# Order of centring, turning and draining in the two channel layer norms of a spectral-convolution and expert block

## The reference, cut to what matters

```python
def _ln_c(v, eps=1e-06):                # over the 32 channels of a pixel
    m = jnp.mean(v, axis=1, keepdims=True)
    s = jnp.var(v, axis=1, keepdims=True)
    return (v - m) / jnp.sqrt(s + eps)

x = x + spectral_conv(_ln_c(x))         # 2D FFT, weights per mode, inverse FFT
t = tokens(x); t = t + experts(_ln_t(t))    # 16 experts, 8 tokens each
x = x + sweeps(_ln_c(x))                # 4 recurrent 1D convolutions over rows and columns
t = tokens(x); t = t + experts(_ln_t(t))
```

## Time and profile before

| | us |
|---|---|
| median of three runs | 591.21 |
| lowest and highest run | 589.81, 595.68 |
| the profiled execution's own time | 595.93 |
| span of that execution, first to last instruction | 594.1 |
| TensorE busy | 551.5 (93%) |
| VectorE busy | 338.5 (57%) |
| ScalarE busy | 305.8 (51%) |

### The profile page before, as it was taken

How to read it: one execution, slowest core, us unless ns; L and a number is a source line. 1 busy time by engine, 2 the same in 40 slices (tenths; PEclk the granted TensorE clock), 3 DMA queues, 4 the chain that set the end, 5 groups by cost and what they waited for, 6 DMA issues and landing times.

```text
span 594.1 us, 26043 instructions
## 1 busy us (share of the span) xinstructions
PE 551.5 (93%) x11064; PEld 514.8 (87%) x11064; DVE 338.5 (57%) x825; ACT 305.8 (51%) x787; POOL 63.6 (11%) x62
## 2 busy tenths in 40 slices
PE   8979989999999799887999999989999999987896
PEld 7979979999998787676999999989999999977782
DVE  3746757657439953873444444434444444379826
ACT  4765746552447611363555555576666555567300
POOL 4000000002012000000000003350000033550000
PEclk9999989999999697996999999999999999999978
DMA  9830765070000000000000004250000144420007
GB/s 354 350 142 1 268 236 212 2 284 1 1 2 1 2 2 20 1 1 1 3 1 0 2 5 106 73 87 4 1 0 1 25 77 72 79 37 1 1 4 282
DMA packets 48157, 40.76 MB, mean 69 GB/s; under 512 B 42554, under 2 KB 42810, under 8 KB 46877
## 3 DMA queue, kind: packets, MB, share of 16 engines
q1 hardware_dynamic: 46606, 37.27, 19.5%
q0 software_dynamic: 1344, 2.17, 1.8%
q10 hardware_dynamic: 144, 0.39, 0.2%
HBM read 27.49 MB, written 4.19 MB: 53 GB/s over the span
## 4 chain that ended last, share of the span: by engine, by line
PE 71%; DVE 17%; ACT 4%; POOL 2%; SPq 2%; issue 2%; DMA 1%; DVEq 0%; ACTq 0%
PE PS L735 33%; PE PS L524 5%; PE PS L470 4%; PE PS L652 3%; PE PS L508 3%; PE PS L728 3%; PE PS L599 2%; PE PS L548 2%; PE PS L555 2%; DVE sums L1041 2%; PE PS L629 2%; DVE RCD L1053 2%; PE PS L569 2%; PE PS L425 2%; PE PS L449 2%
## 5 line engine op out<-in xcount | busy, mean ns | idle before, releaser
L735 PE MATMUL PS<-RE,conv_sb 128*64 128x64 f32 x6048 | 228.8, 228 | 1.9 <-DVE RE L1154 1.4
L735 PEld LDWEIGHTS PS<-RE,conv_sb 128*64 128x64 f32 x6048 | 211.3, 137 | 11.0 <-DVE RE L1154 3.7
L1154 DVE SCALAR_TENSOR_TENSOR RE<-PS,RE 128x64 f32<-128x64 f32 x504 | 113.2, 225 | 123.7 <-PE PS L735 113.7
L728 PE MATMUL PS<-ones_bf,biasT 128*64 128x64 bf16 x1008 | 100.4, 192 | 0.0
L863 ACT ACTIVATE RE<-RCD 128x128 f32 (+1 forms) x126 | 38.9, 310 | 55.7 <-DVE RE L1154 55.6
L728 PEld LDWEIGHTS PS<-ones_bf,biasT 128*64 128x64 bf16 x1008 | 60.0, 112 | 1.0 <-issue 0.2
L470 PE MATMUL PS<-warm 128*128 128x128 bf16 x540 | 42.9, 251 | 5.3 <-DVE ones_bf L922 1.5
L470 PEld LDWEIGHTS PS<-warm 128*128 128x128 bf16 x540 | 39.4, 114 | 6.8 <-ACT RCD L764 1.7
L318 POOL DMA_DIRECT2D RE<-RCD x32 | 18.6, 588 | 190.8 <-ACT RCD L866 190.8
L866 ACT COPY RB<-RE 128x128 f32 (+1 forms) x126 | 35.6, 283 | 1.5 <-DVE RE L1154 1.5
L863 ACT ACTIVATE RE<-RE 128x128 f32 (+1 forms) x63 | 26.6, 422 | 18.8 <-DVE RE L1154 17.6
(11 more groups left out here) (124 smaller groups left out, 791.5 us busy)
## 6 DMA issues: line engine op xcount, KB each, us to landing
RE<-wspec SPq DMA_DIRECT2D x8, 2048.0 KB, 8.6
RA<-x_in SPq DMA_DIRECT2D x8, 512.0 KB, 7.4
RCD<-x_in SPq DMA_DIRECT2D x1, 4096.0 KB, 13.4
out<-RA SPq DMA_DIRECT2D x8, 512.0 KB, 3.5
RCD<-RB SPq DMA_DIRECT2D x48, 64.0 KB, 2.1
RCD<-RB SPq DMA_DIRECT2D x26, 32.0 KB, 1.9
conv_sb<-conv_w SPq DMA_DIRECT2D x1, 768.0 KB, 20.0
RE<-RCD SPq DMA_DIRECT2D x8, 96.0 KB, 4.2
```

The costliest lines, as they stand in the source:

```text
L728: pe.matmul(conv_bank(u, h)[MO * o:MO * (o + 1)], biasT[:, s, MO * o:MO * (o + 1)], ones_bf[:, :], start=True, stop=False)
L735: m = pe.matmul(conv_bank(u, h)[MO * o:MO * (o + 1)], conv_sb[:, s, d, MO * o:MO * (o + 1)], prev, start=False, stop=(d == 2))
L1154: dve.scalar_tensor_tensor(out=state[:, state_slot(s, u), k, 1:1 + HO], in0=conv_bank(u, h), scalar=0.0, in1=rowb[:, u, k], op0=ALU.max, o ...
```

## The change

On TensorE `centre_group(ln, g + 3)` moves from behind `follower(g)` to ahead of it, for g = 1 to 4, in both norms. On ScalarE `drain_follower(g - 3)` moves from ahead of the square of group g to behind that square and the root of group g - 1, for g = 4 to 7. No instruction is added or taken away, no wait changes its value, and VectorE's order stays as it is.

```diff
@@ PE, norm_tokens
                 for g in range(2 * ln, 4):
                     centre_group(ln, g)
                 for g in range(ln, 8):
-                    follower(g)
                     if 1 <= g < 5:
                         centre_group(ln, g + 3)
+                    follower(g)
@@ ACT, norm_tokens
                 for g in range(8):
                     if g == 4 - 2 * ln:
                         drain_follower(0)
-                    if g >= 4:
-                        drain_follower(g - 3)
                     act.wait_ge(s_cen, 8 * ln + g + 1)
                     ...
                     elif g >= 1 + 2 * ln:
                         root(LN0[ln] + g - 1, 32 * (g - 1), 32, eps_sb[:, 0:1])
+                    if g >= 4:
+                        drain_follower(g - 3)
```

## The result

The changed kernel took a median of 602.83 us (601.03 to 605.67, 4 runs) against 590.51 us for the kernel before, measured beside it (588.39 to 595.68, 4 runs). The ratio is 1.0194, 95% interval 1.0158 to 1.023: slower by 9 to 14 us. Forecast were 602.0 us and a range of 595.5 to 609.

What follows compares the result with a forecast made beforehand. TensorE carries 71% of the chain; in the norms, drains, centres and followers would take turns. First norm 5.7, second 1.7 and clock 3.4 sum to +10.8 us on the median 591.21, giving 602.0 us, range 595.5 to 609.

Steps and rivals of the forecast that it cites:

- The ring in the first norm: First norm: drain, centre and follower take turns, 5.77 us per group; gate matmul starts 5.7 us later.
- Square and root cost nothing beside the follower: First norm, ScalarE: square (1.02 us) and root (0.31) ahead of the drain fit beside the follower's 1.95.
- The second norm: Second norm: ScalarE's new order bounds a ring of 4.60 us per group; sweeps start about 1.7 us later.
- The clock: TensorE in both norms: seven new idle gaps bring two falls to half clock, +3.4 us, bounds 0 to 11.9.
- Rival 1: Both norms: ring as worked out but no new clock fall, +7.4 us, 598.6; chance 0.25.
- Rival 2: Both norms: every new idle gap brings a clock fall, +19.3 us, 610.5; chance 0.10.
- Rival 3: Behind both norms: shifted phase keeps the clock up at both tails, +2.9 us, 594.1; chance 0.13.
- Rival 4: Centring groups on TensorE: followers not really late, so kernel faster or equal; chance 0.02.
- The weights' load: SyncE's load after the first norm's last sum: issued at about 40.4 us instead of 34.81, staying hidden.

Runs made afterwards that it cites:

- e3: Changed kernel with 24 dummy bf16 matmuls ahead of each of centres 4 to 7 of the first norm; 599.76 us, ratio 1.0179 to the kernel before.
- e1: Changed kernel with ScalarE's old order put back, so TensorE's new order alone; 610.15 us, ratio 1.0328 to the kernel before.
- e7: Changed kernel with drains 0 to 3 of the first norm split between ScalarE and VectorE; 594.19 us, ratio 1.0022 to the kernel before.
- e2: Changed kernel with TensorE's old order put back, so ScalarE's new order alone; 598.76 us, ratio 1.0133 to the kernel before.
- e6: Kernel before with both halves of the change made in the first norm alone; 600.72 us, ratio 1.0174 to the kernel before.
- e5: Kernel before with both halves of the change made in the second norm alone; 593.13 us, ratio 1.0043 to the kernel before.
- e4: Kernel before with dummy matmuls in both norms' tails and without the 36 warming matmuls of the first sweep; 583.55 us, ratio 0.9856 to the kernel before.
- c1: Kernel before, unchanged, run once more for a second trace; traced run 594.52 us, measured 590.24 us.

## Why the prediction was right

- **The ring in the first norm** was right in place, cause and size: four idles of 2.06 us (2.04 forecast), a turn of 5.87 (5.77), its waits about 6 us (5.7; e3 gives 6.2). The missing 0.1 per turn is in the start after an idle: centre to follower took 27.84 - 25.98 = 1.86, not the 1.78 of matmuls that run on the earlier trace rows, and copy's end to centre 0.14, not 0.06. e1 shows that TensorE's order alone makes it, e7 that the drain is its link.
- **Square and root cost nothing beside the follower**: right for the whole change. e2 shows the other side, where the follower does not cover them.
- **The second norm**: +1.7 forecast at equal clock, 1.6 measured (e6 against the changed kernel). A turn was 4.69 (4.60).
- **The clock**: +3.4 was taken as two falls more than before; the two traces of the changed kernel had three and two in the first norm, 4.7 and 3.0 us by e3's yardstick, and e6 had three. That gaps of 2.06 are not each followed by a fall, and gaps of 1.47 by none, held in both. But the forecast left out that the second tail could gain: there both traces are 2.8 us better than the kernel before, so the net of the clock in the norms is +1.9 and +0.2.
- **Rival 1**, no new fall, which was also what the Trainium skill's "TensorE: Matmul & The Clock Gate" (Why this matters for your kernels) would make of it, falls: all idles were shorter than those it warns of, and the clock fell at 18.9, 32.5 and 39.4 us. **Rival 2** falls with centre 5 in the first trace and centres 4 and 6 in the second, which ran at full clock. **Rival 3** came true in one half: the second tail did run at full clock, worth 2.8 us to that stage (+1.6 of ring, -1.2 measured), but the fall in the transposes stayed. What was held against it, that the waits at both tails remain as long as they are, was wrong: follower 4 now stands behind centre 7 too, and the idle ahead of follower 6 went from 2.94 to 2.05 us in the second norm and from 1.52 to 0.31 in the first. The shorter wait is no guarantee either: after 2.05 or 2.06 us the clock fell in e3, e5 and e7. **Rival 4** falls, since all four centres waited.
- **The weights' load** was issued at 45.34 and not at about 40.4, since the clock delayed it too, and stayed hidden: the third mixing step began 35.8 us after the issue in both kernels (34.81 to 70.58 before, 45.34 to 81.11).
- **Luck in the total**: 602.0 against 602.83 is closer than the account of it. In the traces the two norms together are 9.7 and 7.9 us longer (forecast 10.8): 7.4 us of waits were forecast and about 7.8 measured, 3.4 of clock were forecast and 1.9 and 0.2 measured net. The medians lie 12 us apart, and no trace shows where the rest is. The forecast also added its sum to a median though the clock's falls outside the norms differ from run to run. If the shorter runs of the kernel before had their second tail at full clock, as e6 had, the norms would differ by 12.5 and 10.8 us, but that is a guess. The mean granted clocks on record agree with it without giving the place: 0.959 and 0.966 in the two traced runs of before, 0.968 to 0.979 in those of its runs under 590.5 us that have one on record.

## What to carry to other kernels

When a producer works some groups ahead and shares its slot with a consumer of an earlier group, ask which instruction frees the slot and whether the engine that must wait for it has other ready work ahead of the wait. If the ready work stands behind it, producer, consumer and copy take turns, and the price per group is the sum of their links, here 5.87 us, instead of TensorE's own work, 3.77. Some of the idles that this opens were followed by 3.4 us at half clock. Dummy matmuls ahead of the wait cost nothing here (e3, e4), and those behind it stood on the path, so put them ahead.

## What the runs showed that was not expected

- Whether an idle is followed by 1.2 GHz is not fixed by the idle. Ten of the eleven traces have the 1.96 us ahead of the gate matmul; in six of them the transposes then ran partly at half clock, in c1, e1, e2 and e3 they did not. The 2.94 us of the second norm was followed by a fall in two traces of before and not in e6. The stretches inside the first norm lasted 3.4 us each, the one at the second tail of before about 10, and each costs half its length where TensorE has work.
- The trace of the kernel before showed a tail of 8.88 us from the last square to the sweeps' warming matmuls that I took as given. The second norm's stage became 4.6 us shorter with it filled (2.8 of it by the clock). In the middle of the first norm, which the change set out to reorder, TensorE idled 2.74 us in all.
